# A decoder block in one kernel: query and key stacks handled per unit in six slots instead of per pair in three, with a prologue rebuilt around unit 0

## What is computed

```python
x = x + attn(layernorm(x), w_qkv, w_out)      # windows of 64 queries; keys: own and preceding window, causal
x = x + xattn(layernorm(x), ctx, ctx, mask, Wq, bq, Wk, bk, Wv, bv, Wo, bo)   # all 256 context positions
x = x + ffn(layernorm(x), w1, conv_w, conv_b, w2)  # 128 -> 512, depthwise conv of 3 taps, silu, 512 -> 128,
                                              # activations rounded to int8 steps, weights to -1, 0, 1
```

## Time and profile before

| | us |
|---|---|
| median of 3 runs (lowest, highest) | 323.36 (322.66, 327.88) |
| the profiled execution, its own time | 324.95 |
| its span, first to last instruction | 323.2 |
| busy: PE, DVE, ACT, POOL | 285.6, 231.3, 164.6, 134.4 |
| prologue, to the first beat | 47.7 |
| local iterations 0 to 7 | 47.7 to 151.6 |
| cross iterations and what follows | 151.6 to 323.2 |

### The profile page before, as it was taken

The page is one execution under the profiler, slowest core; times in us unless marked ns, Lnnn a source line. Parts: engine busy times, 40 slices in busy tenths (PEclk is TensorE's granted clock), DMA queues, the critical chain, the costliest instruction groups (busy, mean ns, idle before and its releaser), DMA issues.

```text
span 323.2 us, 8541 instructions
## 1 busy us (share of the span) xinstructions
PE 285.6 (88%) x3298; PEld 183.8 (57%) x3298; DVE 231.3 (72%) x562; ACT 164.6 (51%) x329; POOL 134.4 (42%) x216
## 2 busy tenths in 40 slices
PE   0814899999998997999999999999998999999993
PEld 0712557777775775877656656555554444544551
DVE  7758872567665665689968678786885349999675
ACT  1310016545654562655768677766777753433332
POOL 5633049656486383645869360000016413342000
PEclk9985557999999998899999999999999999999999
DMA  7278538566747653655356274300000000000001
GB/s 256 61 179 206 188 67 187 145 163 164 171 102 221 168 108 100 153 116 130 78 135 133 70 184 100 98 3 1 3 0 3 0 3 1 18 24 17 18 24 32
DMA packets 20135, 30.96 MB, mean 96 GB/s; under 512 B 2812, under 2 KB 17532, under 8 KB 18432
## 3 DMA queue, kind: packets, MB, share of 16 engines
q1 hardware_dynamic: 19368, 29.99, 37.6%
q10 hardware_dynamic: 728, 0.44, 0.5%
HBM read 16.53 MB, written 13.63 MB: 93 GB/s over the span
## 4 chain that ended last, share of the span: by engine, by line
PE 59%; DMA 15%; DVE 12%; ACT 4%; issue 4%; SPq 3%; ACTq 1%; POOL 1%; DVEq 0%
DMA KT<-stack_parts 11%; PE ps L338 9%; PE ps L303 8%; PE ps L268 7%; PE ps L403 6%; DMA QT<-mT 4%; PE ps L351 4%; PE ps L314 3%; SPq L1161 2%; PE ps L272 2%; ACT probs L588 2%; PE ps L362 2%; PE ps L286 2%; PE ps L276 2%; DVE probs L820 2%
## 5 line engine op out<-in xcount | busy, mean ns | idle before, releaser
L740 DVE TENSOR_REDUCE negm<-ps 128x2 bf16<-128x512 f32 (+1 forms) x192 | 124.1, 690 | 56.7 <-PE ps L268 24.2
L588 ACT ACTIVATE probs<-ps 128x512 f32<-128x512 f32 x192 | 105.7, 609 | 35.3 <-PE ps L314 22.9
L303 PE MATMUL ps<-QT,KT 98*128 98x512 bf16 x128 | 47.5, 382 | 4.2 <-ACT probs L588 4.0
L268 PE MATMUL ps<-KT,QT 97*128 97x256 bf16 x256 | 47.5, 272 | 2.4 <-DMA KT<-stack_parts 1.9
L403 PE MATMUL ps<-tapw,xqT 128*128 128x512 f32 x96 | 44.1, 592 | 0.0
L268 PEld LDWEIGHTS ps<-KT,QT 97*128 97x128 bf16 x256 | 23.8, 98 | 17.0 <-DVE negm L740 2.8
L338 PE MATMUL ps<-probs,V 128*32 128x256 f32 x512 | 30.9, 382 | 0.7 <-ACT probs L588 0.7
L986 POOL TENSOR_TENSOR ve<-mv,eps 128x2 f32<-128x2 f32 x8 | 1.6, 194 | 64.1 <-DVE mv L777 64.1
L1041 POOL TENSOR_SCALAR_AFFINE_SELECT probs<-probs 128x512 f32<-128x512 f32 x32 | 21.2, 661 | 14.9 <-ACT probs L588 14.9
L403 PEld LDWEIGHTS ps<-tapw,xqT 128*128 128x128 f32 x96 | 18.2, 190 | 15.0 <-issue 14.3
L626 ACT ACTIVATE probs<-ps 128x512 f32<-128x512 f32 x16 | 9.6, 597 | 33.2 <-PE ps L403 33.2
(11 more groups left out here) (134 smaller groups left out, 502.9 us busy)
## 6 DMA issues: line engine op xcount, KB each, us to landing
stack_parts<-high SPq DMA_DIRECT2D x32, 192.0 KB, 3.3
QT<-stack_parts SPq DMA_DIRECT2D x16, 384.0 KB
KT<-stack_parts SPq DMA_DIRECT2D x8, 768.0 KB
stack_parts<-mid SPq DMA_DIRECT2D x32, 128.0 KB, 3.1
stack_parts<-low SPq DMA_DIRECT2D x32, 64.0 KB, 2.1
CT<-in_ctx_t_dram SPq DMA_DIRECT2D x1, 1024.0 KB, 9.9
out_dram<-probs SPq DMA_DIRECT2D x16, 64.0 KB, 1.5
X<-in_xp_dram SPq DMA_DIRECT2D x1, 768.0 KB, 5.5
```

The costliest lines, as they stand in the source:

```text
L268: last = nc.tensor.matmul(o[:, j * S:(j + 1) * S], QT[r, s, j, pr, e * S + t * P:e * S + (t + 1) * P], KT[r, s, pr, e, :], start=True, sto ...
L303: last = nc.tensor.matmul(o.rearrange("p (j q) -> p j q", j=2), KT[r, s, pr, e, kt * P:(kt + 1) * P], QT[r, s, :, pr, e * S:(e + 1) * S], ...
L588: nc.scalar.activation(probs[:, k, :], bank(n % 3), ACT.Exp, scale=SCALE).then_inc(s_exp, 1)
L740: nc.vector.tensor_reduce(dst, src, AX.X, ALU.max, negate=True).then_inc(m_max, 1)
```

## The change

- A stack now belongs to one unit. QT and KT have six slots of one unit each, the DRAM buffer holds four units, and semaphores count per unit; the part stores have a semaphore for even and for odd units. `store(u, part)` issues 4 DMAs with 512-byte runs, `load(u)` the same three loads at half the size (2 x 192 KB, 384 KB).
- SP's waits for rows of maxima go, but for one ahead of `load(2)`.
- The first stores and loads are written out in a mixed order.
- x comes in four DMAs, the local weights in two. Context and cross weights are loaded behind stack 5, the FFN's weights behind stack 6, its taps behind stack 7.
- VectorE zeroes query slot 0 alone, half the size; GpSimd the five others. VectorE makes mid and low part of unit 0.
- PE gets nine matmuls of 128 x 512 ahead of the first transpose and eight ahead of the transpose of unit 5, whose results nobody reads; units 2 to 4 are projected into banks of their own, without waiting for the bank of an earlier one.
- GpSimd makes the identity first, then query slot 1 and the first statistics, then the masks.
- 14 maxima, not 16, stand ahead of iteration 0, which takes six then.
- All index arithmetic on slots follows (not shown).

```diff
-GROUPS = UNITS // 2
+SLOTS = 6
...
-        return {-1: 16, 0: 20, 1: 30}[i]
+        return {-1: 14, 0: 20, 1: 30}[i]
...
-            return max(0, n - (beats - total))
+            return (0, 1, 2, 2, 2, 3, 4, 5, 6)[n]
...
-        QT = sb("QT", [P, 3, 2, PAIRS, 2 * S], BF16)
-        KT = sb("KT", [P, 3, PAIRS, 2, S], BF16)
+        QT = sb("QT", [P, SLOTS, 2, PAIRS, S], BF16)
+        KT = sb("KT", [P, SLOTS, PAIRS, S], BF16)
...
-        parts = nc.dram_tensor("stack_parts", (2, 2, 2, 6, 64, 2 * S), BF16, kind="Internal").ap()
+        parts = nc.dram_tensor("stack_parts", (4, 2, 2, 6, 64, S), BF16, kind="Internal").ap()
...
-        x_in = [sem(f"x_in{i}") for i in range(2)]
+        x_in = [sem(f"x_in{i}") for i in range(4)]
...
-        part_out = [sem(f"part_stored{i}") for i in range(3)]
-        st_in = [sem(f"stack_in{i}") for i in range(3)]
+        part_out = [[sem(f"part{i}_stored_{e}") for e in range(2)] for i in range(3)]
+        st_in = [sem(f"stack_in{i}") for i in range(SLOTS)]
...
+        def stack_in(u):
+            return 16 * sum(4 if is_cross(e) else 3 for e in range(u % SLOTS, u + 1, SLOTS))
+
+        Q_READY, V_READY, V_ALL = 1, 3, 7
...
-                        pe.wait_ge(st_in[u // 2 % 3], stacks_in(u // 2))
-                        pe.wait_ge(rows_q[u // 2 % 3], 16)
+                        pe.wait_ge(st_in[u % SLOTS], stack_in(u))
+                        pe.wait_ge(rows_q[u % SLOTS], 16)
...
+                def turn_over(count):
+
+                    for _ in range(count):
+                        nc.tensor.matmul(bank(BY), identb[:], identb[:].unsqueeze(1).to_broadcast([P, 4, P]),
+                                         start=True, stop=True)
+
                 pe.wait_ge(s_pc, PC_IDENT)
+                turn_over(9)
                 x_turn(0, bank(6)).then_inc(xT_ps, 1)
-                x_turn(1, bank(7)).then_inc(xT_ps, 1)
                 pe.wait_ge(w_in, 16)
                 qk_project(0, bank(0))
+                x_turn(1, bank(7)).then_inc(xT_ps, 1)
                 qk_project(1, bank(1))
+                pe.wait_ge(wv_in, 16)
                 v_project(0, bank(2))
...
-                pe.wait_ge(rest_done, 1)
-                qk_project(2, bank(0))
-                pe.wait_ge(rest_done, 2)
-                qk_project(3, bank(1))
+                qk_project(2, bank(3))
+                qk_project(3, bank(4))
                 x_turn(4, bank(6)).then_inc(xT_ps, 1)
+                pe.wait_ge(xT_sb, 4)
+                turn_over(8)
                 x_turn(5, bank(7)).then_inc(xT_ps, 1)
-                pe.wait_ge(v_sb, 1)
-                qk_project(4, bank(2))
+                qk_project(4, bank(5))
                 pe.wait_ge(s_pc, PC_ALL)
                 pe.wait_ge(rows_in, 32)
-                for n in range(10):
+                for n in range(8):
+                    if n < 2:
+                        pe.wait_ge(rest_done, 3 + n)
+                    if n == 2:
+                        pe.wait_ge(raw_done, 1)
                     max_unit_mms(n)
                 pe.wait_ge(xT_sb, 5)
                 max_turn(0, bank(BX, BF16))
-                for n in range(10, max_end(-1)):
+                for n in range(8, max_end(-1)):
                     max_unit_mms(n)
                 pe.wait_ge(s_dc, V_ALL)
-                pe.wait_ge(rest_done, 4)
-                pe.wait_ge(raw_done, 1)
+                pe.wait_ge(v_sb, 1)
...
-                act.dma_start(wp[:, 0:4, :].rearrange("p n d -> p (n d)"), wpack[:, 0:4 * D]).then_inc(w_in, 16)
+                act.dma_start(wp[:, 0:2, :].rearrange("p n d -> p (n d)"), wpack[:, 0:2 * D]).then_inc(w_in, 16)
+                act.dma_start(wp[:, 2:4, :].rearrange("p n d -> p (n d)"), wpack[:, 2 * D:4 * D]).then_inc(wv_in, 16)
...
                 ox_copy(0, bank(6), S, 2 * S)
+                high_copy(0, bank(0))
                 ox_copy(1, bank(7), S, 2 * S)
-                high_copy(0, bank(0))
                 high_copy(1, bank(1))
...
-                high_copy(2, bank(0))
-                high_copy(3, bank(1))
+                high_copy(2, bank(3))
                 v_copy(0, bank(2))
+                high_copy(3, bank(4))
...
+                raw_copy(4, bank(5))
                 m_copy(0, bank(BX, BF16))
                 row(0)
-                raw_copy(4, bank(2))
...
+                def first_mid_low():
+
+                    r = raw[:, :, 0:S]
+                    v.wait_ge(rest_done, 1)
+                    nc.vector.tensor_copy(mid[:, :, 0:S], r).then_inc(mid_done, 1)
+                    v.wait_ge(mid_done, 1)
+                    nc.vector.tensor_tensor(low[:, :, 0:S], r, mid[:, :, 0:S], ALU.subtract).then_inc(low_done, 1)
...
                 link(nc.vector.memset(QT[:, 0], 0.0))
                 v.wait_ge(x_in[0], 16)
                 x_stats(0)
+                v.wait_ge(x_in[1], 16)
                 x_stats(1)
                 normalise(0)
                 normalise(1)
-                v.wait_ge(x_in[1], 16)
+                v.wait_ge(x_in[2], 16)
...
+                rest_make(0, bank(0))
+                first_mid_low()
+                rest_make(1, bank(1))
                 normalise(2)
                 normalise(3)
-                rest_make(0, bank(0))
-                rest_make(1, bank(1))
+                v.wait_ge(x_in[3], 16)
...
-                rest_make(2, bank(0))
-                rest_make(3, bank(1))
-                link(nc.vector.memset(QT[:, 1], 0.0))
+                rest_make(2, bank(3))
+                rest_make(3, bank(4))
                 normalise(4)
                 normalise(5)
-                link(nc.vector.memset(QT[:, 2], 0.0))
+                link(nc.vector.memset(V[:, 1], 0.0))
+                link(nc.vector.memset(V[:, 1, :, 0:4:3, HD:HD + 1], 1.0))
...
-                    g.wait_ge(part_out[0], STORED * (u // 2))
+                    g.wait_ge(part_out[0][u % 2], STORED * (u // 2))
...
+                def query_slot(s):
+                    nc.gpsimd.memset(QT[:, s].rearrange("p j r t -> p (j r t)").bitcast(F32), 0.0).then_inc(s_zero, 1)
...
+                query_slot(1)
+                rstd_part(0, 0)
+                rstd_part(1, 2)
...
+                g.wait_ge(low_done, 1)
+                mid_part(1)
+                low_part(1)
+                rstd_part(4, 8)
+                rstd_part(5, 10)
+                query_slot(2)
+                mid_part(2)
+                low_part(2)
+                mid_part(3)
+                low_part(3)
+                query_slot(3)
                 split(4)
+                query_slot(4)
+                query_slot(5)
...
+                def slot_free(u):
+
+                    if u >= SLOTS:
+                        sp.wait_ge(s_ps, before(u - SLOTS + 1))
+                    if is_cross(u):
+                        b = u - B
+                        sp.dma_start(KT[MASK_ROW:MASK_ROW + 1, u % SLOTS],
+                                     mask_r[:, b * S:(b + 1) * S].unsqueeze(1).to_broadcast([1, PAIRS, S])
+                                     ).then_inc(st_in[u % SLOTS], 16)
+                    if u >= 4:
+                        sp.wait_ge(st_in[(u - 4) % SLOTS], stack_in(u - 4))
+
+                def store(u, part):
+                    src, done = ((high, high_done), (mid, mid_done), (low, low_done))[part]
+                    sp.wait_ge(done, u + 1)
+                    for j in range(2):
+                        for n, slots in enumerate((Q_SLOTS[part], K_SLOTS[part])):
+                            step = slots[1] - slots[0] if len(slots) > 1 else 1
+                            sp.dma_start(parts[u % 4, n, j, slots[0]:slots[-1] + 1:step].rearrange("s p t -> p s t"),
+                                         src[64 * j:64 * j + 64, n, u % 2 * S:(u % 2 + 1) * S].unsqueeze(1).to_broadcast(
+                                             [64, len(slots), S])).then_inc(part_out[part][u % 2], 16)
+
+                def load(u):
                     for part in range(3):
+                        sp.wait_ge(part_out[part][u % 2], STORED * (u // 2 + 1))
                     for j in range(2):
+                        sp.dma_start(QT[48 * j:48 * j + 48, u % SLOTS, j].rearrange("p r t -> p (r t)"),
+                                     parts[u % 4, 0, j].rearrange("s (c r) t -> (s c) (r t)", r=PAIRS)).then_inc(st_in[u % SLOTS], 16)
+                    sp.dma_start(KT[0:ROWS, u % SLOTS].rearrange("p r t -> p (r t)"),
+                                 parts[u % 4, 1].rearrange("j s (c r) t -> (j s c) (r t)", r=PAIRS)).then_inc(st_in[u % SLOTS], 16)
+
+                def stack(u):
+                    slot_free(u)
+                    for part in range(3):
+                        store(u, part)
+                    load(u)
+
+                def query_row(s):
+                    if s == 0:
+                        sp.wait_ge(s_dc, Q_READY)
+                    else:
+                        sp.wait_ge(s_zero, s)
```

(45 more changed lines are left out.)

98 lines of the change are left out of this document (24 added, 74 removed).

## The result

The changed kernel took 322.09 us (median of 20 executions, 318.99 to 324.56), the kernel before 324.02 (20, 322.13 to 327.88). The ratio is 0.991 with a 95% interval of 0.9885 to 0.9935: faster by 0.9%, some 2.9 us, inside the 2% band. The ratio and its interval leave out the three executions of the change and the two of before that lie more than 1.5% above the fastest of their kernel; the medians over all twenty differ by 1.9 us. The forecast was 315.9, so the sign is right and the size is not: 322.09 lies above the forecast's own 313 to 319 and just above the whole range.

A forecast was written before the change was run, and what follows sets the result against it. The prediction took the serial prologue of stores and stack loads, then TensorE's waits on stacks, as the bound. Terms -3.6 + 0.8 + 0.3 + 0.5 - 5.5 = -7.5 us gave 315.9 us; own range 313 to 319, whole range 311.5 to 322.

The forecast's parts named there:

- the sum: Whole kernel: the terms -3.6, +0.8, +0.3, +0.5 and -5.5 add up to -7.5 us.
- -3.6: Iteration 0's fifth beat, waiting for unit 2's stack: it lands at 50.3 us against 53.92 before.
- T: Prologue: when SP issues the first store, forecast 10.1 us (9.7 to 11.1) against 14.19 before.
- rival (2): SP's queue: issues stay at 0.77 us, 9.2 a unit, and eat the lead; -3.2 us, 320.2, chance 0.18.
- the 7.9 of the sum: SP's queue: twelve store issues of one unit take 7.9 us, 0.66 each, although each moves half as much.
- the upper half of the bounds: SP's stores per unit, bounds 7.4 to 11.1 us: the upper half if every store keeps its cost at half size.
- +0.8 for the clock: TensorE stands about 2 us for unit 2's stack, then half clock: +0.8 us, the middle of 0 and 1.7.
- +0.3 for late context: Iteration 3: context and cross weights, loaded behind unit 5, land at 79.3 to 80.6, wanted at 81.2; +0.3 us.
- Rival (4): Iteration 3 waits for context, landing up to 4 us late, and the clock falls; -2.1 us, 321.3, chance 0.11.
- +0.5 for a row: Local iterations: one row of maxima meets a load on the shared DMA engines; +0.5 us.
- -5.5 for the later waits: Units 4 to 8: TensorE's waits of 0.55, 1.35 and 1.90 us and 1.7 at half clock go; -5.5 us.
- Rival (3): SP becomes the bound: at 11.1 us per twelve issues unit 8 lands 13.8 us later; 337 us, chance 0.06.

The follow-up runs named there:

- after_look: The changed kernel run once more without any edit, for its trace; one execution, 321.78 us.
- e_early2: Changed kernel with unit 2's stack loaded behind the first four stores of unit 3 instead of all twelve and a row of ones; 322.76 us, ratio 0.995.
- e_preonly: Changed kernel with context and cross weights loaded at the start, SP's order otherwise as in the change; 320.44 us, ratio 0.990.
- e_pre: Changed kernel with unit 2's stack loaded early and context and cross weights both loaded at the start; 316.92 us, ratio 0.978.
- e_warm52: Changed kernel with sixteen matmuls whose result nobody reads while TensorE waits for unit 2's stack; 323.12 us, ratio 0.994.
- the gates: SP waits again for a row of maxima ahead of each load from unit 4 on, added to three edited versions of the change; 331.72, 328.46 and 321.31 us.
- e_pre_taps: As e_pre, with the FFN's taps loaded behind stack 9 instead of stack 7; 316.69 us, ratio 0.977.

## Why the prediction was right or wrong

**The step that failed.** Of the 7.5 us of the sum the ratio shows 2.9. Two places of the sum were too good, by about as much each. The start of iteration 1 was to come 2.8 us earlier (-3.6 + 0.8); it came 0.6 later in the profile and 0.4 earlier in after_look. Iteration 3 was to lose 0.8 (context 0.3, a row 0.5); it lost nothing in the profile and 3.2 in after_look. The later waits gave 0.5 more than forecast. Behind the sizes stands one wrong assumption, that these terms add: as e_early2, e_preonly and e_pre show, the late inputs are a limit that takes back what is won ahead of it.

**T and SP's issues: right in the prologue, too low behind it.** T was 9.20 (10.1 forecast, 9.7 as the lower bound): the statistics began 2.0 us earlier (3.99, not 6.02) and not 1.4. The stores of a unit took 7.9 us in the prologue, as forecast, but 8.5 to 9.6 for units 4 to 7, and from stack to stack SP needed 12.8 to 14.0 us for units 5 to 8, where I had 11.2 to 12 and called 12.3 the limit. That TensorE waited for none of these stacks is owed to SP's lead: the key load of unit 8 was issued at 114.29 and its first maxima ran at 123.14. The 0.77 of rival (2) went with the halved bytes; that it was backlog fits, but isn't shown, as the high parts had more bytes and 0.62. The Trainium skill ("DMA: Bandwidth & Descriptors", Rules for kernel authors) warns that for transfers under 64 KB one pays mostly overhead; the trace agrees in so far as a store of 32 KB holds SP as long (0.60 us) as one of 96 KB (0.62). A cost that stays at half the size is the 7.9 of the sum, and not the upper half of the bounds, as the prediction has it. It cost the DMA engines nothing: the queue's share stayed (37.6% before, 37.7% after) with 36376 packets instead of 20135. GpSimd's memset took 1.81 us (bounds 1.7 and 3.2), beside VectorE's of 1.76 us, without either standing for the other, ended before the first statistics, and cost nothing.

**Load of unit 2, "-3.6": it was -1.8.** From T to its first issue 36.9 us, not 35.2: two loads at 1.45 to 1.5 instead of 1.2, an issue of 1.29, rows of ones at 0.7. From that issue to the landing 6.0, not 5.0, at 234 GB/s with the load of unit 3 right behind it (issued from 47.51 on) and unit 4's stores beside it, where I had taken the middle of 240 and 309 for a load alone. Together 2.7, less the 0.9 by which T was better.

**"+0.8 for the clock": it was +2.4.** I expected a stand of 2 us; it was 3.23, because iteration 0 came as forecast and the stack 1.8 us later. From landing to iteration 1 it took 6.5 us, against 4.1 before. e_warm52 shows all of it as avoidable (4.0 us). The price does not follow the length of the stand: in after_look TensorE stood 4.00 us, kept the full clock for its first matmuls and needed 5.6 us. These two terms are why iteration 1 came 0.6 us later than before, not 2.8 earlier.

**"+0.3 for late context": the main error.** I priced it as a small delay behind an iteration 3 at 81.2. The transfers were later than forecast (81.6 and 82.2, not 79.3 to 80.6), since SP reached them at 73.97 and not 71.3, and they are a floor, by their own landing or by the row that they slow: whatever the prologue wins above it is given back, as e_early2 shows with 2.35 us of wait, half clock behind it, and no gain. Rival (4) named this mechanism; I had it as one of two outcomes of chance, while it is what binds as soon as the first step goes as forecast. In the profile of the change itself no wait appears at iteration 3, as the first floor stands just as high: the row was in 0.3 us ahead, the weights 2.2. A trace without a wait had not shown that there was slack.

**"+0.5 for a row": 0 to 3.2.** Nothing in the profiled execution, 1.42 us of wait and its slow clock (3.2 us) in after_look. The row of iteration 3 is sent while context and weights are under way, so it is the same place again. They are not its only company: with both at the start it still took 5.6 us in e_pre, beside stack 5 and unit 6's stores, and 3.4 in e_preonly.

**"-5.5 for the later waits": right.** From iteration 1 to 7 the profiled execution took 6.0 us less. Rival (3), SP as the bound, didn't happen, but SP's 12.8 to 14.0 us a unit and the gates show how near it is.

The sum over the typical trace: iteration 1 at -0.4, iterations 1 to 7 -6.0 + 3.2 = -2.8, together -3.2, and the ratio's 0.9% is 2.9 us. The forecast's 316 us was reached by e_pre (316.92), with order and placement that the change doesn't have.

**Open.** Of the change there are two traces, at 319.63 and 321.78 us; what makes an execution one of 324 was not seen. A first store at 10.3 to 10.6 instead of 9.2, as in three other traces, may be a part of it. How much of the second floor is the inputs' own landing and how much the slowed row was not separated. The rebuilt prologue and the one-unit stacks were not run apart. The 1.6 us at 134.3 in e_pre_taps have no cause that I can name.

## What to carry to other kernels

When a transfer is moved from the start to behind other work, compute its landing, and that of every small transfer it slows, as a floor for everything after its first use, and take the saving as the smaller of what is won before it and its slack; two floors of one height hide each other in every single-edit experiment, so lift them together before you call either harmless. Bulk loads that are wanted late belong where the queue is idle, at the start, and not beside the small row that an engine waits for. A wait on the issuing queue that keeps bulk from a small transfer costs more than the late row once that queue has no slack.

## What the runs showed of the hardware that was not expected

- A store's issue on SP had one median price, 0.60 to 0.62 us, for 32, 64 and 96 KB, and the same for 192 KB before the change; with the outliers twelve of them took 7.9 us in the prologue and up to 9.6 later.
- A row of 8 KB, 1.8 us on free engines, took 6 to 7 us with 1 to 2 MB under way on the other queue (6.2 in after_look, 7.0 in e_warm52), and 4.5 us at the same place in the profile of the change.
- After a stand of 3.23 us TensorE had the 1.2 GHz level for 4.5 us of dense work; that cost 2.4 us against the 1.7 that I took for a stand of 1.90. A stand of 4.00 us in after_look cost 1.6, and sixteen matmuls during the stand in e_warm52 saved all of it.
- The same nine fillers ahead of the first projection left it at 0.67 us in the profile of the change and at 1.19 in three of fifteen traces, where the first store came 1.1 to 1.4 us later.
